# Mamba-2 mixer with a mixture-of-experts block on one core: z and output projections as three split products, one convolution tap moved from DVE to ACT and POOL, a new order on every engine

## The chip, the core and the metric

The kernel runs on one core of a Trainium2 chip. A time is the device time of one execution in microseconds (us); several executions are given by their median. The profile is of one execution. PE is TensorE (matmul), PEld its weight load, DVE is VectorE, ACT is ScalarE, POOL is GpSimd and SP is SyncE, which here only issues transfers.

## The reference, cut to what matters

Four sequences of 2048 tokens, 512 wide. A layer norm with a modulation, a Mamba-2 mixer (in-projection, a convolution of four taps, a chunked state-space scan of 16 heads, a gate, an out-projection), a second layer norm, and 64 experts of which each token takes eight, with a shared expert.

```python
h = _layernorm(x) * (1 + ca) + sa
# mixer
xn = h * rsqrt(mean(h * h) + EPS) * norm_w
zxbcdt = einsum("bld,ed->ble", xn, in_proj_w)      # z: 1024, xBC: 1024 + 128 + 128, dt: 16
conv = sum(pad[:, k:k + l, :] * conv_w[:, k] for k in range(4)) + conv_b
xBC = conv * sigmoid(conv)
dt = softplus(dt + dt_bias)
y = _ssd(xh * dt[..., None], dt * A, Bm, Cm) + D * xh       # chunks of 128 tokens
y = y * (z * sigmoid(z))
y = y * rsqrt(mean(y * y) + EPS) * gnorm_w
x = x + ga * (h + einsum("bld,ed->ble", y, out_proj_w))
# feed-forward
h = _layernorm(x) * (1 + cb) + sb
x = x + gb * (routed_experts(h) + shared_expert(h))
```

All inputs and outputs are float32.

## The kernel before

The program has three parts, each an unrolled loop or a loop over blocks of 128 tokens: `mixer` (64 chunks of 128 tokens), `experts` (576 blocks) and `combine` (64 blocks). The change touches `mixer` alone.

`mixer` is a software pipeline written by hand. A step `s` works on several chunks at a time: chunk `e = s + 2` gets its first layer norm, chunk `f = s + 1` its in-projection, convolution and gate, chunk `c = s` its scan and out-projection, chunk `t = s - 1` its second layer norm and its routing, and chunk `q = s - 2` has its token numbers scattered to the experts' lists (eight indirect DMAs that POOL issues). Each engine has a function `step` that issues its instructions for all of these chunks in the written order; nothing reorders them. Engines wait for each other by the semaphores in `S`. So a step takes as long as the slowest loop through the engines' queues, and the mixer takes about 64 such steps.

One step on each engine, in its written order:

- PE: the small products of `c` (L766 to L769), the transposes of `xr` (L775), the row sums of the decay matrix `lm` (L788), the xBC projection (L811, 40 matmuls) with the transposes of `h2` for routing (L795) in it, dt (L815), the router (L825), the scan (L832, L844, L853), the z projection (L860, eight float32 matmuls of 512 columns), the transposes of `y` (L867), the ranks, the transposes of `xbc` (L881) and the out-projection (L888, eight float32 matmuls of 512 columns).
- DVE: the residual `x1` and its statistics (L1109 to L1119, written at the end of `step`, but they run at the turn of a step), the small scan terms (L940, L944), `x1s` (L949), the decay matrix times C·B (L956), half of the splitting of the expert weights (`split_lo`, L518), three taps of the convolution for ten tiles (L982, 30 instructions), dt (L991, L993), the routing (L998 to L1037) with the terms of the softplus series between its instructions, the chain of `y` and the state (L1043 to L1056), `xbc` (L1059), gates and places, and `split_lo` again.
- POOL: `xg` (L587, L590), the two norms' powers and their scalings (L594 to L621), the elementwise products of the scan (L601, L627, L633), and the eight list DMAs (L645).
- ACT: copies from PSUM, exponentials, the first tap (L701), tanh, the upper halves of the expert weights (`split_hi`).

In the experts, and only there, a product is made of float32 operands that are split into an upper and a lower part of the type float32r: `split_products` adds hi·hi, hi·lo and lo·hi, three matmuls for one.

Of the kernel before, what the change touches and what calls it, by code (L numbers as in the profile page):

```python
# [4 lines left out]
FP32 = mybir.dt.float32  # L5
# [19 lines left out]
DIN = 2 * DI + 2 * P + NH  # L25
EXPERTS, TOPK, FF = 64, 8, 256
# [134 lines left out]
def mixer(nc, top, sem, tile, bank, half, env):  # L161
# [11 lines left out]
    with ExitStack() as ph:  # L173
# [9 lines left out]
        a_neg = sb("a_neg", [P, NH])  # L183
        d_skip = sb("d_skip", [P, NH])
# [25 lines left out]
        with ExitStack() as st:  # L210
# [7 lines left out]
            pad_id = tile(st, "pad_id", [P, P], I32)  # L218
            w_mod_dh = w_mod_d.rearrange("p k (a n) -> p k a n", a=2)
# [8 lines left out]
                     (w_router, w_router_d), (b_router, b_router_d), (w_in, w_in_d)]  # L228
            with nc.Block() as block:
                @block.sync  # L230
                def _(sp):
                    sp.dma_start(c_in[:], c_t).then_inc(s_cin, 16)
                    for a in range(2):
                        if a:
                            for dst, src in loads:
                                sp.dma_start(dst[:], src).then_inc(s_load, 16)
                            sp.wait_ge(s_pe_set, 3)
                        sp.dma_start(w_mod[:].rearrange("p k a n -> p k (a n)"),
                                     w_mod_dh[:, :, a, :]).then_inc(s_wmod[a], 16)
                    sp.dma_start(w_out[:], w_out_d).then_inc(s_wout, 16)  # L240
# [5 lines left out]
                    sp.wait_ge(s_row, 16)  # L246
                    for b in range(2):
                        sp.dma_start(mod[:, b, :, :].rearrange("p m d -> p (m d)"),
                                     mod_dram[b:b + 1, 0:5 * DM].broadcast_to([P, 5 * DM])).then_inc(s_bcast, 16)
                    sp.wait_ge(s_bcast, 16 * 2)  # L250
# [43 lines left out]
                def _(act):  # L294
                    act.wait_ge(s_const, 8)
                    act.dma_start(h2_dram[TOKENS:TOKENS + P, :], zeros[:]).then_inc(s_zero, 16)
                    act.wait_ge(s_cin, 16)
                    nc.scalar.activation(c_tanh[:], c_in[:], ACT.Tanh, scale=0.5).then_inc(s_act_set, 1)
                    act.wait_ge(s_load, 16 * len(loads))
# [5 lines left out]
                    for k in range(KD):  # L305
                        nc.scalar.activation(w_in[:, k, 0:DIN // 2], w_in[:, k, 0:DIN // 2], ACT.Copy,
                                             scale=norm_w[:, k:k + 1]).then_inc(s_act_set, 1)
                    act.wait_ge(s_wout, 16)
                    for k in range(KI):
                        nc.scalar.activation(w_out[:, k, :], w_out[:, k, :], ACT.Copy,  # L310
# [14 lines left out]
                def _(dve):  # L325
# [13 lines left out]
                    for k in range(KD):  # L339
                        nc.vector.tensor_scalar(w_in[:, k, DIN // 2:DIN], w_in[:, k, DIN // 2:DIN],  # L340
                                                norm_w[:, k:k + 1], None, ALU.mult)
# [25 lines left out]
                    nc.vector.tensor_copy(mod_abs[:, 0:1], mod_row[:, 0, 0:1]).then_inc(s_setup, 1)  # L367

        RT = 3 * P
        XGROUPS = 4  # L370
        OLD = TAPS - 1
        passed = sem("passed")
        SH_A, SC_A, G_A, SH_B, SC_B = range(5)
# [10 lines left out]
        junk = sb("junk", [P, DI], mybir.dt.bfloat16)  # L384
# [6 lines left out]
        xbc = sb("xbc", [P, 2, NE, P])  # L391
        gz = sb("gz", [P, 2, DI])
# [23 lines left out]
        y_t = sb("y_t", [P, KI, P])  # L416
# [1301 lines left out]
```

## Time and profile before

| | |
|---|---|
| median of 3 runs | 5845.8 us (5838.91 to 5846.02) |
| profiled execution, its own time | 5848.36 us |
| its span, first to last instruction | 5846.6 us |
| mean granted TensorE clock | 0.986 of full speed |
| busy, share of the span | PE 96%, PEld 73%, DVE 62%, POOL 60%, ACT 45% |

The mixer fills the first 2700 us or so, the experts most of the rest. In the mixer DVE and PE are both nearly always busy; in the experts PE is, and DVE falls to four tenths. A share over the whole span therefore says little on the mixer, and the rows further down are taken from single steps of it. A step is there about 40 us long. "Busy" on DVE or POOL includes time in which an instruction has been started and is held up, so a long duration of a short instruction is a wait too.

### The profile page before, as it was taken

Reading aid. Unit: us, or ns where it says so; the run is one execution under the profiler, and the core shown is the slowest. Engines: PE = TensorE matmul, PEld = TensorE weight load, DVE = VectorE, ACT = ScalarE, POOL = GpSimd, SP = SyncE. Lnnn points to the kernel's source line nnn. Section 1 sums busy time; section 2 is a strip of 40 time slices with the busy share of each in tenths; the row PEclk is TensorE's granted clock in tenths of the full one; section 3 lists DMA queues with packets and bytes.
Section 4 is the critical chain, followed back from the end, with each engine's and each line's share of the span. In section 5 each row is a group of like instructions: output and inputs, shape, how many; then the busy total and the mean of one; then the engine's idle time right before and its main releaser. Section 6 shows DMA issues by size and latency. Waiting matters only on the chain.

```text
span 5846.6 us, 109797 instructions
## 1 busy us (share of the span) xinstructions
PE 5613.9 (96%) x28797; PEld 4286.0 (73%) x28798; DVE 3597.2 (62%) x10033; ACT 2627.2 (45%) x5588; POOL 3535.2 (60%) x2980
## 2 busy tenths in 40 slices
PE   5999999999999999994999999999999999999999
PEld 3666666666666666663888888887888888888887
DVE  4889888888898898883444444443444444444454
ACT  3555555555555555551333333333333333333322
POOL 2667667667676676673555555554555555555587
PEclk8999999999999999996999999999999999999999
DMA  5443444444444444343688788778678778878687
GB/s 203 163 149 144 162 155 152 154 143 163 158 145 165 147 146 160 145 151 133 138 225 222 183 202 224 164 177 238 138 182 203 160 161 218 208 199 201 132 277 248
DMA packets 340193, 1028.38 MB, mean 176 GB/s; under 512 B 57109, under 2 KB 61461, under 8 KB 339173
## 3 DMA queue, kind: packets, MB, share of 16 engines
q1 hardware_dynamic: 194232, 703.53, 32.9%
q0 software_dynamic: 145568, 321.56, 28.1%
q8 instruction: 118, 1.93, 0.1%
q14 instruction: 131, 1.07, 0.1%
q10 hardware_dynamic: 144, 0.29, 0.0%
HBM read 580.45 MB, written 444.74 MB: 175 GB/s over the span
## 4 chain that ended last, share of the span: by engine, by line
PE 52%; DMA 1%; POOL 0%; issue 0%; DVE 0%; SPq 0%; ACT 0%; POOLq 0%; ACTq 0%
PE bank L1244 45%; PE bank L1379 4%; PE bank L1386 2%; PE bank L1573 0%; PE bank L1582 0%; DMA w_lo<-lo_dram 0%; POOL acc_c L1555 0%; DMA h_c<-h_dram 0%; DMA lst_i<-list_dram,row 0%; DMA xg_e<-h_dram,ids 0%; POOL o_c L1559 0%; POOL acc_c L1546 0%; DMA acc_dram<-y_e,ids 0%; POOL lst_i L1172 0%; SPq L1531 0%
## 5 line engine op out<-in xcount | busy, mean ns | idle before, releaser
L1360 POOL DMA_INDIRECT acc_dram<-y_e,ids x576 | 910.4, 1580 | 1113.1 <-ACT y_e L1432 789.1
L1244 PE MATMUL bank<-w_hi,x_hi 128*128 (+1 forms) x2560 | 1056.1, 413 | 1.7 <-DVE x_lo L1647 1.2
L1244 PE MATMUL bank<-w_hi,x_lo 128*128 (+1 forms) x2560 | 1000.8, 391 | 0.0
L1244 PE MATMUL bank<-w_lo,x_hi 128*128 (+1 forms) x2560 | 1000.7, 391 | 0.0
L1450 DVE TENSOR_TENSOR h_lo<-bank,h_hi 128x256 fp32r<-128x256 f32 x576 | 243.8, 423 | 763.9 <-ACT h_hi L1421 763.7
L1432 ACT ACTIVATE y_e<-bank,xg_e 128x512 f32<-128x512 f32 x576 | 396.4, 688 | 698.4 <-PE bank L1244 698.4
L645 POOL DMA_INDIRECT list_dram<-tok_id,pos x512 | 594.9, 1162 | 156.0 <-issue 154.8
L1352 POOL DMA_INDIRECT xg_e<-h_dram,ids x576 | 571.0, 991 | 193.9 <-issue 174.9
L1426 ACT ACTIVATE th_f<-bank 128x256 f32<-128x256 f32 x576 | 221.3, 384 | 1011.2 <-PE bank L1244 1011.2
L811 PEld LDWEIGHTS bank<-xn_t,w_in 128*128 128x128 f32 x5120 | 587.8, 190 | 67.0 <-ACT btok L687 65.4
L811 PE MATMUL bank<-xn_t,w_in 128*128 128x131 f32 x5120 | 605.4, 276 | 14.8 <-ACT btok L687 14.1
L1459 DVE SCALAR_TENSOR_TENSOR hs_f<-th_f,bank 128x256 f32<-128x256 f32 x576 | 242.7, 421 | 600.1 <-ACT th_f L1426 599.8
L1244 PEld LDWEIGHTS bank<-w_hi,x_lo 128*128 128x128 f32 x2560 | 481.3, 188 | 103.5
L1244 PEld LDWEIGHTS bank<-w_hi,x_hi 128*128 128x128 f32 x2560 | 482.8, 189 | 83.4 <-DVE x_lo L1647 1.4
L1244 PEld LDWEIGHTS bank<-w_lo,x_hi 128*128 128x128 f32 x2560 | 484.1, 189 | 79.1
L982 DVE SCALAR_TENSOR_TENSOR acc<-bank,conv_w,acc 128x128 f32<-128x128 f32 x1920 | 505.7, 341 | 8.5 <-ACT acc L701 8.4
L1244 PE MATMUL bank<-w_hi,h_hi 128*128 (+1 forms) x1280 | 499.5, 390 | 2.2 <-DVE h_lo L1450 1.3
L1244 PE MATMUL bank<-w_hi,h_lo 128*128 (+1 forms) x1280 | 500.0, 391 | 0.0
L1244 PE MATMUL bank<-w_lo,h_hi 128*128 (+1 forms) x1280 | 498.1, 389 | 0.0
L888 PE MATMUL bank<-w_out,y_t 128*128 128x512 f32 x1024 | 452.4, 595 | 1.2 <-ACT y_t L751 1.2
L860 PE MATMUL bank<-w_in,xn_t 128*128 128x512 f32 x1024 | 450.0, 592 | 0.9 <-DVE acc L982 0.9
L1455 DVE TENSOR_TENSOR x_lo<-bank,x_hi 128x512 fp32r<-128x512 f32 x576 | 392.1, 681 | 8.7 <-ACT x_hi L1416 8.7
(247 smaller groups left out, 10448.6 us busy)
## 6 DMA issues: line engine op xcount, KB each, us to landing
hi_dram<-w_hi_m SPq DMA_DIRECT2D x130, 768.0 KB, 3.3
lo_dram<-w_raw SPq DMA_DIRECT2D x130, 768.0 KB, 4.8
w_hi<-hi_dram SPq DMA_DIRECT2D x130, 768.0 KB, 7.4
w_lo<-lo_dram SPq DMA_DIRECT2D x130, 768.0 KB, 10.2
w_raw<-in_w_experts_dram SPq DMA_DIRECT2D x128, 768.0 KB, 5.0
acc_dram<-zeros SPq DMA_DIRECT2D x130, 256.0 KB, 2.8
acc_c<-acc_dram SPq DMA_DIRECT2D x128, 256.0 KB, 3.5
h_dram<-h SPq DMA_DIRECT2D x64, 288.0 KB, 4.1
```

Of the source, the lines that this page charges most:

```text
L645: pool.indirect_dma_start(list_dram, bass.IndirectOffsetOnAxis(ap=pos[:, p, k:k + 1], axis=0), tok_id[:, p:p + 1], None).then_inc(list_st[ ...
L811: last = nc.tensor.matmul(raw_of(i), w_in[:, k, m:m + P], xn_t[:, k, :], start=(k == 0), stop=(k == KD - 1))
L860: last = nc.tensor.matmul(half(j), xn_t[:, k, OLD:], w_in[:, k, j * 512:(j + 1) * 512], start=(k == 0), stop=(k == KD - 1))
L888: last = nc.tensor.matmul(half(7), y_t[:, i, :], w_out[:, i, :], start=(i == 0), stop=(i == KI - 1))
L982: last = stt(out=acc[:, i, :], in0=raw_of(i)[:, k:k + P], scalar=conv_w[:, i, k:k + 1], in1=acc[:, i, :], op0=ALU.mult, op1=ALU.add)
L1244: last = nc.tensor.matmul(acc, a, b, start=(i == 0), stop=(i == len(terms) - 1))
L1352: pool.indirect_dma_start(xg[:, r, :], None, h2_dram, bass.IndirectOffsetOnAxis(ap=ids[:, r:r + 1], axis=0)).then_inc(g_in[r], 16)
L1360: pool.indirect_dma_start(acc_dram[r % NACC], bass.IndirectOffsetOnAxis(ap=ids[:, r:r + 1], axis=0), y[:, r % YSLOTS, :], None, compute_op ...
L1432: nc.scalar.activation(y[:, r % YSLOTS, :], half(6 + r % 2), ACT.Copy, scale=xg_flat[:, bass.ds(e + (r * ROW + DM), 1)]).then_inc(S["y_sb" ...
L1450: nc.vector.tensor_tensor(h_lo[:, r, :], half(4 + r)[:, 0:KF * P], h_hi[:, r, :].bitcast(FP32), ALU.subtract).then_inc(S["hT_lo"], 1)
L1455: nc.vector.tensor_tensor(x_lo[:, r, :], half(r), x_hi[:, r, :].bitcast(FP32), ALU.subtract).then_inc(S["xT_lo"], 1)
L1459: nc.vector.scalar_tensor_tensor(out=hs[:, r, :], in0=th[:, r, :], scalar=1.0, in1=half(2 + r)[:, 0:FF], op0=ALU.add, op1=ALU.mult).then_i ...
```

## The change

z and output projections. The weights of z and of the output are split once, at the start, into `wz_hi`, `wz_lo`, `wo_hi`, `wo_lo`; each step splits `xn` and `y` (upper part copied by ACT, lower part subtracted by DVE), and PE multiplies by three float32r matmuls in place of each float32 one: 48 in place of 16 in a step.

Convolution. DVE's three taps become two. ACT multiplies the second tap into a new tile `acc2` (ten more instructions in a step) and POOL adds `acc2` to `acc` (one instruction of 128x1280).

Order and buffers. The small products and terms of a chunk move from the start of its step to the end of the one before. The residual `x1` moves to the start of the next step. The C·B matrix goes into an SBUF tile `cbm`, where before it stayed in PSUM. `xbc` and `gz` have one buffer in place of two, `y` lies in `acc2`, `y_hi` and `y_lo` share memory with `x1s` and `x2s`, `tmp_s` is gone (POOL scales `state` in place). The modulation rows lie in three tiles of which two are loaded for one batch at a time; the zeros for the accumulators are read from a 128x128 tile by a repeating pattern; both halves of the weight splitting stand at the end of a step on DVE.

```diff
@@ ACT, convolution, one group of four @@
-                        for i in group(g):
-                            last = nc.scalar.activation(acc[:, i, :], raw_of(i)[:, 0:P], ACT.Identity,
-                                                        bias=conv_b[:, i:i + 1], scale=conv_w[:, i, 0:1])
+                        for i in group(0):
+                            nc.scalar.activation(acc2[:, i, :], raw_of(i)[:, 1:1 + P], ACT.Copy, scale=conv_w[:, i, 1:2])
+                            last = nc.scalar.activation(acc[:, i, :], raw_of(i)[:, 0:P], ACT.Identity, bias=conv_b[:, i:i + 1], scale=conv_w[:, i, 0:1])
...
@@ POOL @@
+                        pool.wait_ge(S["taps"], XGROUPS * (f + 1))
+                        nc.gpsimd.tensor_tensor(acc[:], acc[:], acc2[:], ALU.add).then_inc(S["csum_done"], 1)
...
-                        nc.gpsimd.tensor_tensor(heads(tmp_s[:]), heads(state[:]), per_head(etk[:]),
-                                                ALU.mult).then_inc(S["tmps_done"], 1)
+                        pool.wait_ge(S["yoff_ps"], c + 1)
+                        nc.gpsimd.tensor_tensor(heads(state[:]), heads(state[:]), per_head(etk[:]), ALU.mult).then_inc(S["tmps_done"], 1)
@@ PE @@
-                        for j in range(2):
-                            pe.wait_ge(S["taps"], XGROUPS * f + 2 - j)
-                            for k in range(KD):
-                                last = nc.tensor.matmul(half(j), xn_t[:, k, OLD:], w_in[:, k, j * 512:(j + 1) * 512],
-                                                        start=(k == 0), stop=(k == KD - 1))
-                            last.then_inc(S["z_ps"], 1)
+                        pe.wait_ge(S["taps"], XGROUPS * f + 2)
+                        pe.wait_ge(S["xn_lo"], f + 1)
+                        split_products(nc, half(0), [lambda k, t=t: t[:, k, :] for t in (xn_hi, xn_lo)],
+                                       [lambda k, t=t: t[:, k, 0:512] for t in (wz_hi, wz_lo)], KD).then_inc(S["z_ps"], 1)
...
-                        for i in range(KI):
-                            last = nc.tensor.matmul(half(7), y_t[:, i, :], w_out[:, i, :], start=(i == 0), stop=(i == KI - 1))
-                        last.then_inc(S["out_ps"], 1)
+                        first = [(y_hi, k, w) for k in range(KI) for w in (wo_hi, wo_lo)]
+                        for i, (a, k, w) in enumerate(first):
+                            nc.tensor.matmul(half(7), a[:, k, :], w[:, k, :], start=(i == 0), stop=False)
...
+                        pe.wait_ge(S["ylo_done"], c + 1)
+                        for k in range(KI):
+                            last = nc.tensor.matmul(half(7), y_lo[:, k, :], wo_hi[:, k, :], start=False, stop=(k == KI - 1))
+                        last.then_inc(S["out_ps"], 1)
@@ DVE @@
+                        tt(xn_lo[:], xn_t[:, :, OLD:], xn_hi[:].bitcast(FP32), ALU.subtract).then_inc(S["xn_lo"], 1)
...
-                            tt(heads(lm[:, j * DI:(j + 1) * DI], 8, P), heads(lm[:, j * DI:(j + 1) * DI], 8, P),
-                               half(4)[:, 0:P].unsqueeze(1).to_broadcast([P, 8, P]), ALU.mult).then_inc(S["m_done"], 1)
+                        tt(heads(lm[:, 0:DI], 8, P), heads(lm[:, 0:DI], 8, P),
+                           cbm[:].unsqueeze(1).to_broadcast([P, 8, P]), ALU.mult).then_inc(S["m_done"], 1)
...
-                            for k in range(1, TAPS):
+                        for k in range(K1, TAPS):
...
+                        if c + 1 < NCH:
+                            dve.wait_ge(S["csum_done"], c + 2)
...
+                        tt(y_lo[:].rearrange("p k t -> p (k t)"), bank[2][:], y_hi[:].rearrange("p k t -> p (k t)").bitcast(FP32), ALU.subtract).then_inc(S["ylo_done"], 1)
```

In the order of the instructions two places matter. The first is POOL's queue from the first power of a step to its list DMAs; `ve` and `mv` are the norms' statistics from DVE, `pos` are the places from the routing. Before:

```order
L587 TENSOR_TENSOR xg<-h,mod 128x512 [waits h_done,x1_done]
L590 TENSOR_TENSOR xg<-xg,xin 128x512 [waits x_in0,xg_half]
L594 TENSOR_TENSOR rs<-ve,minus_half 128x1 [waits hn2_done,ln2_var]
...
L619 TENSOR_TENSOR h<-hn,mod 128x512 [waits xr_done,hn_done]
L621 TENSOR_TENSOR h<-h,mod 128x512 [waits h_half]
L627 TENSOR_TENSOR x2s<-x1s,eacs 128x1024 [waits states_ps,exps,x1s_done]
L633 TENSOR_TENSOR tmp_s<-state,etk 128x1024 [waits state_done,etk_done]
L638 TENSOR_SCALAR rre<-ssq 128x1 [waits ssq_done]
L640 TENSOR_TENSOR rr<-rre,minus_half 128x1 [waits rr_var]
L645 DMA list_dram<-tok_id,pos 540672x1 [waits pos_done]
```

And with the change, from the list DMAs of one step to the last large product of the next:

```order
L697 DMA list_dram<-tok_id,pos 540672x1 x7
L632 TENSOR_TENSOR rs<-ve,minus_half 128x1 [waits hn2_done,ln2_var]
...
L647 TENSOR_TENSOR h<-hn,mod_b 128x512 [waits h2T_ps,h2_st0,hn2_done]
L649 TENSOR_TENSOR h<-h,mod_b 128x512 [waits h2_half]
L652 TENSOR_TENSOR xt<-xt,d_skip 128x1024 [waits x1s_done]
L657 TENSOR_TENSOR x2s<-x1s,eacs 128x1024 [waits states_ps,out_ps,exps,x1s_done]
L663 TENSOR_TENSOR xg<-h,mod_g 128x512 [waits h_done,x1_done]
L666 TENSOR_TENSOR xg<-xg,xin 128x512 [waits x_in0,xg_half]
L668 TENSOR_TENSOR acc<-acc 128x1280 [waits taps]
L673 TENSOR_TENSOR state<-state,etk 128x1024 [waits yoff_ps,state_done,etk_done]
L680 TENSOR_TENSOR h<-hn,mod_a 128x512 [waits xg_half,xr_done,hn_done]
L682 TENSOR_TENSOR h<-h,mod_a 128x512 [waits h_half]
```

`xg` moved from the head of the queue to behind `x2s`, the sum of the taps stands behind it and waits for DVE's last tap, the scaling of the state waits for PE's `yoff`, and the scalings of `h` for the first norm come last.

The second place is DVE's queue between the first norm's statistics and the routing. Before (`split_lo` is the row on `w_raw`):

```order
L949 TENSOR_TENSOR x1s<-xt,dt 128x1024 [waits x2s_done,dt_done,xt_sb]
L952 TENSOR_SCALAR etk<-eacs,ends 128x16 [waits tmps_done,exps]
L956 TENSOR_TENSOR lm<-lm,bank 128x1024 [waits l_exp] x2
L961 BN_STATS st<-xin 128x6 [waits x_in1]
L964 BN_AGGR mv<-st 128x2 [waits ln1_stat,dve_e]
L966 TENSOR_SCALAR ve<-mv 128x1 [waits dve_e]
L518 TENSOR_TENSOR w_raw<-w_raw,w_hi_m 128x1536 [waits w_hi]
L982 SCALAR_TENSOR_TENSOR acc<-bank,conv_w,acc 128x128 [waits tap0]
```

With the change:

```order
L1040 TENSOR_SCALAR ve<-mv 128x1 [waits dve_e]
L1045 TENSOR_TENSOR xn_lo<-xn_t,xn_hi 128x512 [waits z_ps,xn_hi]
L1049 TENSOR_TENSOR lm<-lm,cbm 128x1024 [waits cb_done,l_exp]
L1056 TENSOR_TENSOR x1s<-xt,dt 128x1024 [waits ydiag_ps,x2s_done,out_ps,dt_done,xt_sb]
L1066 SCALAR_TENSOR_TENSOR acc<-bank,conv_w,acc 128x128 [waits tap0]
...
L1075 TENSOR_TENSOR lm<-lm,cbm 128x1024 [waits cb_done,l_exp]
L1079 TENSOR_SCALAR etk<-eacs,ends 128x16 [waits tmps_done,exps]
L1083 TENSOR_TENSOR sp_x<-bank,dt_bias 128x16 [waits tap0]
L1085 SCALAR_TENSOR_TENSOR sp_a<-sp_x 128x16 [waits dt_raw]
L1093 SCALAR_TENSOR_TENSOR acc<-bank,conv_w,acc 128x128 [waits tap0]
```

The products with C·B read `cbm` in place of a PSUM bank and stand apart, `xn_lo` is new, `split_lo` has left this stretch for the end of the step, and the two taps that are left are 20 instructions in two pieces.

## Rows read from the trace of the kernel before

**Rows 1.** PE in one step of the mixer: start, duration, line, tiles, idle before.

```profile
1508.24 1.09 PE L867 MATMUL bank<-ident,y 128*128 128x128 f32 x8 [0.62 <-DVE y L1056]
...
1509.64 1.09 PE L881 MATMUL bank<-ident,xbc 128*128 128x128 f32 x8 [0.25 <-DVE xbc L1059]
1510.57 7.03 PE L888 MATMUL bank<-w_out,y_t 128*128 128x512 f32 x16
1517.44 0.38 PE L766 MATMUL bank<-xbc 128*128 128x128 f32 x2
...
1522.43 8.37 PE L811 MATMUL bank<-xn_t,w_in 128*128 128x131 f32 x72 [0.22 <-ACT btok L687]
...
1548.42 1.09 PE L867 MATMUL bank<-ident,y 128*128 128x128 f32 x8 [0.63 <-DVE y L1056]
```

**Rows 2.** PE in one block of the experts: split products, 512 columns each.

```profile
4004.80 0.39 PE L1244 MATMUL bank<-w_lo,x_hi 128*128 x1
...
4008.46 0.39 PE L1244 MATMUL bank<-w_hi,h_lo 128*128 x1
```

**Rows 3.** Waits of DVE from 1000 to 1400 us: total, times, longest.

```profile
DVE x L1109 <- PE bank L888: 27.2, 10, 2.7
```

**Rows 4.** DVE by line, 1000 to 1400 us, ten steps: busy, mean ns, idle before.

```profile
L982 DVE SCALAR_TENSOR_TENSOR acc<-bank,conv_w,acc 128x128 f32<-128x128 f32 x300 | 79.0, 341 | 0.0
L518 DVE TENSOR_TENSOR w_raw<-w_raw,w_hi_m 128x1536 fp32r<-128x1536 f32 x20 | 36.2, 1812 | 0.0
L956 DVE TENSOR_TENSOR lm<-lm,bank 128x1024 f32<-128x1024 f32 x20 | 23.5, 1218 | 2.0 <-ACT lm L691 2.0
L1047 DVE TENSOR_TENSOR y<-y,bank 128x1024 f32<-128x1024 f32 x10 | 12.2, 1222 | 1.1
L1111 DVE TENSOR_TENSOR x<-x,xg 128x512 f32<-128x512 f32 x10 | 6.9, 692 | 0.3
```

**Rows 5.** DVE and POOL side by side in one step: start, duration.

```profile
1520.55 1.26 POOL L590 TENSOR_TENSOR xg<-xg,xin 128x512 f32<-128x512 f32 x1
...
1520.83 1.02 DVE L944 TENSOR_TENSOR acs<-acs 128x16 f32<-128x16 f32 x1
...
1526.70 1.87 DVE L518 TENSOR_TENSOR w_raw<-w_raw,w_hi_m 128x1536 fp32r<-128x1536 f32 x1
1527.03 2.67 POOL L609 TENSOR_TENSOR h<-h,mod 128x512 f32<-128x512 f32 x1
...
1536.06 1.90 POOL L633 TENSOR_TENSOR tmp_s<-state,etk 128x1024 f32<-128x1024 f32 x1
...
1536.51 1.48 DVE L993 SCALAR_TENSOR_TENSOR sp_a<-sp_x 128x16 f32<-128x16 f32 x1
```

**Rows 6.** POOL by line, 1000 to 1400 us, ten steps.

```profile
L645 POOL DMA_INDIRECT list_dram<-tok_id,pos x80 | 93.2, 1166 | 24.8 <-issue 24.8
L601 POOL TENSOR_TENSOR xt<-xt,d_skip 128x1024 f32<-128x1024 f32 x10 | 19.0, 1904 | 0.0
L613 POOL TENSOR_TENSOR rs<-ve,minus_half 128x1 f32<-128x1 f32 x10 | 5.5, 546 | 0.0
```

**Rows 7.** The routing, the chain of y and the end of a step.

```profile
1537.91 0.18 DVE L998 TENSOR_SCALAR sc<-trt 128x64 f32<-128x64 f32 x1
...
1539.10 1.08 POOL L645 DMA_INDIRECT list_dram<-tok_id,pos  x1 [0.18 <-issue]
...
1542.30 1.21 DVE L1043 TENSOR_TENSOR y<-bank,eacs 128x1024 f32<-128x1024 f32 x1
...
1548.28 1.49 DVE L1059 SCALAR_TENSOR_TENSOR xbc<-xbc,acc 128x1280 f32<-128x1280 f32 x1
...
1553.34 1.75 DVE L518 TENSOR_TENSOR w_raw<-w_raw,w_hi_m 128x1536 fp32r<-128x1536 f32 x1
```

**Rows 8.** Mixer's last steps, by stretch: PE, PEld, DVE, ACT, POOL busy, PEclk, DMA, GB/s.

```profile
2650.20:2653.80 3.60, 0.00 (x0) 0.00 (x0) 2.26 (x2) 0.00 (x0) 3.52 (x3) 0.51 0.37 152
2653.80:2667.30 13.50, 12.79 (x48) 10.76 (x49) 3.49 (x24) 2.17 (x3) 11.20 (x10) 0.50 0.26 100
```

More of the change, by code:

```diff
@@ L183, in mixer @@
         a_neg = sb("a_neg", [P, NH])
+        cbm = sb("cbm", [P, P])
         d_skip = sb("d_skip", [P, NH])
@@ L733, in step @@
                     if f is not None:
[L734 to L736 removed]
+                        act.wait_ge(S["z_ps"], 2 * f + 2)
+                        nc.scalar.activation(gz[:, 512:1024], half(1), ACT.Tanh, scale=0.5).then_inc(S["z_th"], 1)
                     if e is not None:
@@ L792, in transposes @@
+                    if c is not None:
+                        pe.wait_ge(S["xt_sb"], c + 1)
+                        pe.wait_ge(S["l_in"], 2 * c + 2)
+                        for i in range(2):
+                            at = DI + i * 512
+                            last = nc.tensor.matmul(half(2 + i), above[:], lm[:, at:at + 512], start=True, stop=True)
+                        last.then_inc(S["rows_ps"], 1)
+                    if t is not None:
                         pe.wait_ge(S["h2_done"], t + 1)
@@ new lines, in step @@
+                        for k in range(K1, TAPS):
+                            for hf in range(2):
+                                if k == K1:
+                                    dve.wait_ge(S["tap0"], XGROUPS * f + hf + 1)
+                                else:
+                                    conv.wait(2 * (k - K1 - 1) + hf + 1)
+                                for i in group(hf):
+                                    last = stt(out=acc[:, i, :], in0=raw_of(i)[:, k:k + P], scalar=conv_w[:, i, k:k + 1],
+                                               in1=acc[:, i, :], op0=ALU.mult, op1=ALU.add)
+                                if k == TAPS - 1:
+                                    last.then_inc(S["taps"], 1)
+                                else:
+                                    conv.mark(last)
@@ L1074, in step @@
                     if f is not None:
+                        for n in range(0 if t is None else SERIES_IN_ROUTE, SERIES):
+                            series(n)
+                        dve.wait_ge(S["z_th"], 2 * f + 1)
+                        stt(out=gz[:, 0:512], in0=gz[:, 0:512], scalar=1.0,
+                            in1=half(0), op0=ALU.add, op1=ALU.mult).then_inc(S["gz_done"], 1)
                         softplus.wait()
```

660 lines of the change are left out of this document (378 added, 282 removed).

## Prediction

> **What bounds the kernel now.** The page says that PE is busy 96% of the span, but that is an average over two stages, so I went to one step of the mixer. On PE the reader is to see how little is missing: the transposes of `y` start at 1508.24 and again at 1548.42, a step of 40.18 us, and PE waits in it for 0.62 + 0.25 + 0.22 = 1.09 us [rows 1]. Next come DVE's waits: it waits in each step 2.72 us for the out-projection, and for nothing else that counts [rows 3]. So a step is one loop through both engines: PE's out-projection, DVE's long queue from `x1` to the chain of `y`, PE's transposes. DVE has 40.18 - 2.72 = 37.46 us of it, PE 39.09.
>
> Last I laid DVE and POOL side by side, since DVE's own time holds hidden waits [rows 5]. `acs` is 16 columns wide and takes 1.02 us: it is over at 1521.85, and the POOL addition beside it, from SBUF, at 1521.81. `sp_a`, as small, takes 1.48 and is over at 1537.99, POOL's product at 1537.96. In the other direction POOL's 512-column addition L609 takes 2.67 where L590, of the same form, takes 1.26: it starts under `split_lo`, which ends at 1528.57, and needs 1.13 more. All these DVE instructions read two SBUF operands. The taps, which read one from PSUM, run in those very microseconds undisturbed: 79.0/300 = 0.263 each [rows 4]. So two-SBUF instructions of DVE and POOL's products exclude each other for a whole instruction, either way. Before, this costs DVE (1.02 - 0.18) + (1.48 - 0.18) = 2.14 us a step, taking the 0.18 of `sc` as a small instruction's price. It costs no more because the routing, with its many small two-SBUF instructions, starts at 1537.91, and POOL turns to the list DMAs at 1539.10 [rows 7]; routing and the chain of `y` run under these.
>
> **The change part by part.**
>
> PE. In the experts 16 split products in a row start 3.66 us apart, 0.229 each [rows 2], so three are 0.686. The eight float32 products take 1517.44 - 1510.57 = 6.87, 0.859 each [rows 1]. Sixteen are replaced: 16 x 0.173 = 2.8 us. PE's loop is then 39.09 - 2.8 = 36.3.
>
> DVE, undisturbed: 37.46 - 2.14 = 35.3. Ten taps less are -2.63 [rows 4]. `xn_lo` costs 0.69 as the `x1` addition, `y_lo` 1.22 as the like-shaped addition from PSUM [rows 4]. For the small terms, now behind 16 matmuls of the out-projection (3.66), and one more dependent pair in the chain of `y`, I add 0.8, an estimate between 0.3 and 1.5. That gives 35.4. Were nothing else to happen, a step would be 36.3 to 36.8.
>
> POOL. `tmp_s` becomes `state`, same size, and the sum of the taps is new: 1.90 x 1280/1024 = 2.38 [rows 6]. Its queue now cannot start its products before DVE has the second norm's variance, since that norm's power is first behind the list DMAs. From that moment, call it 0, POOL has to do: four small steps of the norms 1.6 (0.55 a power), six 512-column products 7.6 (1.26 each), three of 1024 columns 5.7, the sum 2.4; 17.3, with some 1.2 between them 18.5 [rows 5, 6]. DVE undisturbed would from 0 do statistics (about 1.1), `xn_lo` 0.7, `lm` 1.2, `x1s` 1.2, twelve taps 3.2, `lm` 1.2, small ones 0.6, eight taps 2.1, and reach the routing at 11.3. The routing is 4.4 long (1537.91 to 1542.30 [rows 7]) and would be done at 15.7. So POOL is still multiplying in all of it.
>
> The price of that. `xn_lo`, two `lm` and `x1s` are 4.3 us of two-SBUF work that cannot lie beside POOL's 18.5; the two `lm` are new in this, since C·B lay in PSUM and now lies in `cbm`. POOL is then done at up to 22.8. The routing and the series between its instructions need the port eleven times (scores, group sums, comparisons, masks, weights, six of the series). Each of these waits for the POOL instruction in progress, and gets in between two of them. In the eight or so POOL instructions left, about five of the eleven get through; what is left, 2.0 us, follows. The routing ends at 24.8 in place of 15.7: 9.1 lost. If DVE gets on better, so that POOL is kept off for half of the 4.3 and only 1.0 is left over, it ends at 21.7: 6.0 lost. I take 8.4, nearer to the upper end, because in each of [rows 5] the loser waits for the whole instruction. The Trainium skill has this in "SBUF — State Buffer", section "Who interferes with whom": a DVE instruction with two SBUF inputs contends with a GpSimd instruction that reads SBUF, whichever comes second stands still until the first is done, and one with at most one SBUF input does not contend. The trace agrees (0.84 and 1.30 lost beside 0 for the taps). It also condemns the `lm` products, of which no row shows a conflict, since they had a PSUM operand. Without them in it the loss would be 8.4 - 2.4 = 6.0, and the time near 6100.
>
> The clock. PE's loop of 36.3 then has 7 us of waiting in a step of 43.8, most of it in one piece before the transposes of `y`, where it waits for DVE today [rows 1]. In the mixer's tail, where PE stands still for 3.6 us, it is granted 0.51 there and 0.50 in the 13.5 us of work that follow [rows 8], the lower of its two levels, 1.2 GHz. From the transposes of `y` to the small products PE has 2.3 + 3.7 = 6 us of work, and DVE waits for these. Cost: nothing, if the clock is back at once, to 6.0, if it stays down all this way; I take 2.7.
>
> ACT gets eleven instructions more, and is the idlest of the compute engines over the span (45%); SP's transfers, the four times smaller pieces of the zeros, two splittings at the start (8 x 0.69 on DVE, beside the load of the modulation rows) and one more empty step I set at nothing. If that cover fails, they cost some 10 us once.
>
> Sum: 35.4 + 8.4 + 2.7 = 46.5 us a step in place of 40.18, +6.3. About 63 of the 68 steps are full ones: +398 on the profiled execution's own 5848.4 (it is 2.6 above the median shown), so 6246, say 6250.
>
> **The rivals.**
>
> Port without clock: 43.8 a step, +3.6, 6075. For it: PE's work after an idle piece may be spread enough for the clock to come back early. Against: [rows 8].
>
> Faster, the port bites less. Only instructions that meet a long POOL product wait (the second `lm` behind `xt`, `sp_a` behind `x2s`: some 1.4 + 1.5, and 0.6 elsewhere), and the routing slips between POOL's instructions. Then 38.9 a step, -1.3, 5766. It decides at a loss of 40.18 - 35.4 = 4.8 us a step: under that the change is faster. For it: no row shows the routing beside POOL products. Against: `acs` and `sp_a` are as small as the routing's instructions and waited.
>
> Faster, PE's loop alone bounds: the holds stay as small as today's in total, DVE keeps ahead, 36.8 a step, -3.4, 5634. For it: DVE's undisturbed 35.4 is under PE's 36.3. Against: POOL's 18.5 us from moment 0 are longer than DVE's 15.7.
>
> Slower still: the clock stays down for the whole 6.0 us, and the loss is the full 9.1: 50.5, 6500.
>
> **How the numbers follow.** Port and clock 0.50 (on its own 6100 to 6420), port without clock 0.20, the port bites less 0.10, PE alone 0.15, slower still 0.05. A measurement tells about 0.2%, 12 us, from no change. The faster cases give 0.08 of the 0.10 and all of the 0.15: 0.23; same 0.02; slower 0.75. The range leaves out PE alone and the slowest, 0.20: 5760 to 6420.
>
> **What the profile of the changed kernel would show.** If right: small instructions of the routing and the series (`swb`, `gs`, `sp_s`, `sp_q`, `gcmp`) on DVE with durations near 1 us or more, ending together with POOL's `acc`, `state` or `h`; `lm` or POOL's products lengthened by the other; PE waiting some microseconds for `y`; the granted clock under 1.00 through the mixer; steps of 44 to 48 us. The split products should start 0.23 us apart at full clock, whichever case it is. If DVE's small instructions stay near 0.2 us and PE's waits under 1 us a step, the port was not the point and I am wrong by some 600 us. Wrong, too, if POOL's products are over before the routing starts: then moment 0 is earlier than I put it.

## The result and the profile after

| | before | after |
|---|---|---|
| median | 5843.8 us (5838.91 to 5846.02, 4 runs) | 6284.0 us (6278.31 to 6289.44, 4 runs) |
| ratio | | 1.0754, 95% interval 1.0736 to 1.0773 |
| span of the profiled execution | 5846.6 us | 6285.6 us |
| mean granted TensorE clock | 0.986 | 0.937 |

The median before has one run more than the one further up. One run of the versions below, 6250 us with the skip product on ACT, counts as slow and is left out of its median and its ratio.

The change costs 440 us. The page's rows of busy time and of the granted clock, after:

```profile
PE 5643.3 (90%) x29821; PEld 4635.8 (74%) x29822; DVE 3961.6 (63%) x9533; ACT 2829.9 (45%) x6356; POOL 3821.8 (61%) x3044
PEclk8989989989888998998889999999999999999999
```

DVE and POOL are as busy as before, in share; PE's share has fallen from 96% to 90%, and the clock is under full in the first half, the mixer. To see where the time lies, take DVE's product for `xbc`, which stands once in each step. The columns are count, duration in ns (least, median, longest), first and last start. First before, then after:

```profile
L1059 DVE SCALAR_TENSOR_TENSOR xbc<-xbc,acc x64: 1481/1484/1493, 99.0 to 2633.6; 128x1280 f32<-128x1280 f32 x64
```

```profile
L1167 DVE SCALAR_TENSOR_TENSOR xbc<-xbc,acc x64: 1476/1484/2579, 94.8 to 3077.0; 128x1280 f32<-128x1280 f32 x64
```

64 starts are 63 steps: (2633.6 - 99.0)/63 = 40.23 us before, (3077.0 - 94.8)/63 = 47.34 after. 63 x 7.11 = 448 us; behind the last step both kernels need 3213 and 3209 us. So all of the loss is in the mixer's step. (Steps of the kernels below are worked out in the same way.)

Three of the 63 steps, where a new sequence begins, take 53.3, 52.6 and 53.9 us; the other 60 take 47.04 on the mean. In each of the three POOL's `h` waits for the modulation rows of the new sequence (total, times, longest wait):

```profile
POOL h L647 <- DMA mod_b<-mod_dram: 19.7, 3, 7.7
```

They make up 19 us of the 448. The kernel before has no step over 40.7 us behind its second.

In one step, DVE from its wait for the small products into the routing (start, duration, idle before):

```profile
1512.18 0.19 DVE L1218 COPY acs<-bank 128x32 f32<-128x32 f32 x1 [3.73 <-PE bank L965]
...
1519.05 0.15 DVE L1031 TENSOR_SCALAR ve<-mv 128x1 f32<-128x1 f32 x1
...
1527.18 1.60 DVE L1075 TENSOR_TENSOR lm<-lm,cbm 128x1024 f32<-128x1024 f32 x1 [0.87 <-ACT lm L771]
1528.70 1.87 DVE L1079 TENSOR_SCALAR etk<-eacs,ends 128x16 f32<-128x16 f32 x1
...
1533.79 0.18 DVE L1103 TENSOR_SCALAR sc<-trt 128x64 f32<-128x64 f32 x1
1534.00 2.91 DVE L1105 TENSOR_TENSOR swb<-sc,b_router 128x64 f32<-128x64 f32 x1
1536.84 1.89 DVE L992 TENSOR_SCALAR sp_r<-sp_u 128x16 f32<-128x16 f32 x1
...
1540.22 1.13 DVE L998 TENSOR_TENSOR sp_s<-sp_u,sp_r 128x16 f32<-128x16 f32 x1
...
1544.03 1.23 DVE L1152 TENSOR_TENSOR acc<-bank,eacs 128x1024 f32<-128x1024 f32 x1
```

And POOL in the same stretch of time:

```profile
1519.29 0.57 POOL L632 TENSOR_TENSOR rs<-ve,minus_half 128x1 f32<-128x1 f32 x1 [1.87 <-DVE ve L1031]
...
1527.66 2.88 POOL L657 TENSOR_TENSOR x2s<-x1s,eacs 128x1024 f32<-128x1024 f32 x1
...
1533.94 2.89 POOL L668 TENSOR_TENSOR acc<-acc 128x1280 f32<-128x1280 f32 x1 [0.84 <-DVE acc L1093]
1536.79 1.90 POOL L673 TENSOR_TENSOR state<-state,etk 128x1024 f32<-128x1024 f32 x1
...
1540.03 1.28 POOL L682 TENSOR_TENSOR h<-h,mod_a 128x512 f32<-128x512 f32 x1
```

Add start and duration to see which instructions end together. `etk` is over at 1530.57, POOL's `x2s` at 1530.54. `swb`, 64 columns wide, takes 2.91 and is over at 1536.91, the sum of the taps at 1536.83. `sp_r` is over at 1538.73, `state` at 1538.69; `sp_s` at 1541.35, `h` at 1541.31. The routing, 4.4 us before [rows 7], takes 1544.03 - 1533.79 = 10.2.

The groups of DVE's lines from 1000 to 1400 us (count, busy, mean ns) say that every step is like that:

```profile
L1105 DVE TENSOR_TENSOR swb<-sc,b_router 128x64 f32<-128x64 f32 x9 | 26.2, 2910 | 0.3
L1079 DVE TENSOR_SCALAR etk<-eacs,ends 128x16 f32<-128x16 f32 x9 | 16.8, 1867 | 0.0
L1075 DVE TENSOR_TENSOR lm<-lm,cbm 128x1024 f32<-128x1024 f32 x9 | 14.4, 1601 | 7.8 <-ACT lm L771 7.8
L992 DVE TENSOR_SCALAR sp_r<-sp_u 128x16 f32<-128x16 f32 x9 | 13.5, 1504 | 0.0
L1085 DVE SCALAR_TENSOR_TENSOR sp_a<-sp_x 128x16 f32<-128x16 f32 x9 | 10.0, 1116 | 0.3
L998 DVE TENSOR_TENSOR sp_s<-sp_u,sp_r 128x16 f32<-128x16 f32 x9 | 9.6, 1067 | 0.0
L1112 DVE TENSOR_TENSOR gs<-g 128x8 f32<-128x8 f32 x9 | 8.1, 896 | 0.3
L1121 DVE CAST gidf<-gidx 128x8 f32<-128x8 uint32 x9 | 3.7, 407 | 0.0
```

The time that such an instruction takes beyond its own price is called a hold here. With 0.18 us as the price of a small instruction and 1.22 of `lm`, the means give 2.73 + 1.69 + 0.38 + 1.32 + 0.94 + 0.89 + 0.72 + 0.23 = 8.9 us of holds in a step, 2.1 before.

The waits of the same stretch (total, times, longest):

```profile
ACT gz L803 <- DVE acc L1161: 76.3, 8, 9.7
POOL rre L685 <- ACT hn L808: 72.7, 8, 9.3
...
PE bank L937 <- DVE state L1164: 53.8, 8, 7.2
...
DVE acs L1218 <- PE bank L965: 24.9, 8, 3.8
```

The two largest, of ACT and POOL, end with the chain of `y`; ACT's is at the tile `gz`, which has one buffer now. Whether anyone is held up by them is tried below. PE waits 53.8/8 = 6.7 us a step for `y` and the state, DVE 24.9/8 = 3.1 for the small products behind PE's transposes. PE by stretches of one step (length, busy of PE, PEld, DVE, ACT, POOL, then the granted clock):

```profile
1495.50:1502.80 7.30, 0.00 (x0) 0.01 (x1) 6.75 (x11) 1.17 (x3) 0.00 (x0) 0.71 0.00 1
1502.80:1508.80 6.00, 5.98 (x24) 5.45 (x25) 5.30 (x19) 5.20 (x10) 4.72 (x7) 0.51 0.26 96
1508.80:1513.90 5.10, 5.10 (x27) 4.21 (x27) 1.72 (x4) 4.16 (x15) 3.88 (x5) 1.00 0.05 2
```

PE stands still for 7.3 us; the next 6.0, the transposes and the first part of the out-projection, are granted 0.51, the lower level, and then it is back at 1.00.

### The profile page after: what moved, and what is told of

Same layout as the page of the kernel before. It is cut to its first block and busy times, and to the rows that moved or that the text cites. A ratio compares the mean times of both kernels' runs of the same rounds, so it can differ in the third digit from the quotient of the medians.

```text
span 6285.6 us, 113210 instructions
## 1 busy us (share of the span) xinstructions
PE 5643.3 (90%) x29821; PEld 4635.8 (74%) x29822; DVE 3961.6 (63%) x9533; ACT 2829.9 (45%) x6356; POOL 3821.8 (61%) x3044
## 5 line engine op out<-in xcount | busy, mean ns | idle before, releaser
L697 POOL DMA_INDIRECT list_dram<-tok_id,pos x512 | 619.7, 1210 | 155.8 <-issue 154.7
L937 PE MATMUL bank<-ident,acc 128*128 128x128 f32 x512 | 118.7, 410 | 390.4 <-DVE state L1164 390.4
L937 PEld LDWEIGHTS bank<-ident,acc 128*128 128x128 f32 x512 | 95.9, 215 | 416.9 <-issue 416.9
L685 POOL TENSOR_SCALAR rre<-ssq 128x1 f32<-128x1 f32 x64 | 69.4, 1085 | 535.0 <-ACT hn L808 535.0
L1527 ACT CAST x_hi<-bank 128x512 fp32r<-128x512 f32 x576 | 332.8, 578 | 67.5 <-PE bank L1490 67.4
L1490 PE MATMUL bank<-ident,xg_e 128*128 128x128 f32 x2304 | 346.6, 273 | 17.7 <-SPq L1443 8.0
## 6 DMA issues: line engine op xcount, KB each, us to landing
w_lo<-lo_dram SPq DMA_DIRECT2D x130, 768.0 KB, 10.2
```

What stands on the lines that cost most here:

```text
L697: pool.indirect_dma_start(list_dram, bass.IndirectOffsetOnAxis(ap=pos[:, p, k:k + 1], axis=0), tok_id[:, p:p + 1], None).then_inc(list_st[ ...
L937: last = nc.tensor.transpose(bank[2][:, i * P:(i + 1) * P], y[:, i * P:(i + 1) * P], ident[:])
L1490: last = nc.tensor.transpose(half(r % 2)[:, k * P:(k + 1) * P], xg[:, r, k * P:(k + 1) * P], ident[:])
L1527: nc.scalar.copy(x_hi[:, r, :], half(r)).then_inc(S["xT_hi"], 1)
```

## The experiments

Theory: DVE and POOL hold each other up, since POOL's products now reach into the routing (8.9 us a step), and PE's idle piece costs half the clock (2 to 3 us). Rivals: the single buffers and the waits on them; DVE's mere amount of work; the split products on PE. All edits are made to the changed kernel. In the cuts of the edits below `...` stands for lines left out. What was measured, the ratios against the kernel before, the step of the profiled execution:

| edit | median us | ratio, 95% interval | us a step |
|---|---|---|---|
| none (the change) | 6284.0 | 1.0736 to 1.0773 | 47.34 |
| gate tile in two buffers | 6287.7 | 1.0742 to 1.0777 | 47.32 |
| list DMAs earlier | 6289.1 | 1.0750 to 1.0786 | 47.28 |
| POOL's products cut short | 6079.2 | 1.0384 to 1.0419 | 44.17 |
| sum of the taps on DVE | 6212.2 | 1.0616 to 1.0651 | 46.13 |
| second tap back on DVE | 6148.5 | 1.0504 to 1.0539 | 45.03 |
| sum on DVE, state on ACT | 6113.0 | 1.0442 to 1.0477 | 44.52 |
| the same, skip product on ACT | 6154.8 | 1.0468 to 1.0536 | 45.62 |
| sum on DVE, C·B in PSUM, lists earlier | 6138.6 | 1.0489 to 1.0525 | 44.97 |
| tap on DVE, C·B in PSUM, lists earlier | 6299.5 | 1.0762 to 1.0798 | 47.66 |
| PE's idle time filled | 6331.6 | 1.0817 to 1.0853 | 48.01 |
| z in float32 | 6315.5 | 1.0791 to 1.0827 | 47.74 |
| tap on DVE, state on ACT, small terms off the port | 6079.9 | 1.0380 to 1.0415 | 44.17 |

**The rivals first.** The gate tile in two buffers:

```diff
-        gz = sb("gz", [P, DI])
+        gz = sb("gz", [P, 3, 512])
...
-                        at_least(act, S["y_done"], f)
-                        nc.scalar.activation(gz[:, 0:512], half(0), ACT.Tanh, scale=0.5).then_inc(S["z_th"], 1)
+                        at_least(act, S["y_done"], f - 1)
+                        nc.scalar.activation(gz[:, p, :], half(0), ACT.Tanh, scale=0.5).then_inc(S["z_th"], 1)
...
```

> The first half of the gate tile gz gets a second buffer again, so that ACT's tanh into it does not wait for the product of y with the gate (9.5 us a step in the changed kernel), and POOL not for ACT behind it (9.3 us); xr lies in hn to make room, and DVE's product y x gate is two instructions of 512 columns. Port theory: these waits end with the chain of y and hold nobody up, 6284 us, 25 more or less. Theory of the single buffers: 2 us a step or more come back, under 6160 us.

6288: no change. ACT's wait is now at the next instruction that needs `y`, 6.8 us a step for 9.5, POOL's is 7.0 for 9.1, and PE waits as before:

```profile
POOL r2e L690 <- ACT hn L814: 56.1, 8, 7.3
PE bank L940 <- DVE state L1168: 54.1, 8, 7.1
ACT hn L814 <- DVE acc L1165: 54.1, 8, 7.0
```

So more than 2 us of these waits went and nothing was gained: that buffer is not the cause. (Of the other shared buffers none was tried alone.) The list DMAs, moved from the end of POOL's step to behind `h`:

> POOL's eight list DMAs of a step move from its end to behind the last large product h (as before the change, where they ran under the routing). Port theory: POOL's products still cannot start before moment 0 and are as long, so the routing still lies beside them: 6284 us, 60 more or less. Rival, that the routing is only held because the list DMAs left it and pushed the products into it: the holds go, 4 us a step or more, under 6040 us.

6289: no change. POOL then waits for the second norm's variance 94.3/9 = 10.5 us a step, where it waited 0.8: its products can't start sooner, whatever stands ahead of them.

**POOL's products in the routing.** First both made short: the sum is made for one tile of ten, the scaling of the state for one head of sixteen, and the rest of both is left out:

```diff
-nc.gpsimd.tensor_tensor(acc[:], acc[:], acc2[:], ALU.add).then_inc(S["csum_done"], 1)
+nc.gpsimd.tensor_tensor(acc[:, 0:1, :], acc[:, 0:1, :], acc2[:, 0:1, :], ALU.add).then_inc(S["csum_done"], 1)
...
-nc.gpsimd.tensor_tensor(heads(state[:]), heads(state[:]), per_head(etk[:]), ALU.mult).then_inc(S["tmps_done"], 1)
+nc.gpsimd.tensor_tensor(heads(state[:])[:, 0:1, :], heads(state[:])[:, 0:1, :], per_head(etk[:])[:, 0:1, :], ALU.mult).then_inc(S["tmps_done"], 1)
```

> Two POOL instructions are cut short: the sum of the taps is made for one tile of ten, and the scaling of the state for one head of sixteen (that part of the convolution and of the state is left out). POOL loses about 4.4 us of product time in the routing. Port theory: the holds of swb (2.7) and sp_r (1.7) go and those behind h come earlier; 4 to 6 us a step less, 5900 to 6040 us. Theory of the single buffers or of the waits on ACT: no change above 1 us a step, 6220 us or more.

3.2 us a step came back, less than the 4 to 6 expected, and far more than the rival's 1. DVE's instructions are the same ones. Then work was moved without leaving any out. The sum behind DVE's last tap:

```diff
-                        nc.gpsimd.tensor_tensor(acc[:], acc[:], acc2[:], ALU.add).then_inc(S["csum_done"], 1)
...
+                        dve.wait_ge(S["taps"], XGROUPS * (f + 1))
+                        tt(acc[:], acc[:], acc2[:], ALU.add).then_inc(S["csum_done"], 1)
```

> The sum of the two tap tiles (128x1280) is made by DVE behind its last tap, not by POOL. Port theory: DVE gets about 1.5 us of work, but the hold of swb (2.7 us, ended by that POOL sum) goes, and POOL's later products end about 2.5 us earlier against the routing, so that part of the other holds (sp_r 1.7, gs 0.5, sp_s 1.0) goes too: 1 to 4 us a step less, 6030 to 6220 us. Theory that DVE's amount of work decides: 1.5 us a step more, about 6380 us. Theory of the single buffers: 6284 within 20 us or a little more.

DVE does 1.5 us more, and the step is 1.2 us shorter. `swb` is a small instruction again:

```profile
L1099 DVE TENSOR_TENSOR acc<-acc 128x1280 f32<-128x1280 f32 x8 | 11.9, 1492 | 0.3
L1105 DVE TENSOR_TENSOR swb<-sc,b_router 128x64 f32<-128x64 f32 x8 | 1.8, 226 | 0.3
```

The convolution put back whole (`K1 = 1`, no `acc2` product, no sum):

> Only the convolution is put back: the second tap on DVE (ten instructions of 0.26 us that read PSUM), no second tap tile on ACT and no sum on POOL. Port theory: DVE's own work is 2.6 us longer, and of the 9.3 us of holds a step the 2.7 under the sum and part of those behind it go, as with the sum on DVE (6.2 us of holds left there, 46.1 us a step): 44.5 to 47 us a step, 6105 to 6265 us. Theory that only DVE's amount of work counts: 2.6 us a step more than the changed kernel, 6450 us.

6149: DVE has ten instructions of 0.26 us more, and the step is 2.3 us shorter. That DVE's amount of work decides is refuted twice. Next, with the sum on DVE, the state's scaling went to ACT as well:

```diff
...
+                        for hh in range(NH):
+                            last = nc.scalar.activation(state[:, hh * HD:(hh + 1) * HD], state[:, hh * HD:(hh + 1) * HD], ACT.Copy, scale=etk[:, hh:hh + 1])
+                        last.then_inc(S["tmps_done"], 1)
```

> The sum of the taps on DVE, and the scaling of the state by ACT instead of POOL (16 instructions of 128x64, behind the convolution's tanh, where ACT waits 9.5 us for y). Port theory: the 1.9 us that POOL's product of the state held DVE's routing go as well; against the kernel with the sum on DVE (46.1 a step, 6212) 1.5 to 3 us a step less, 6020 to 6120 us. Theory that DVE's small instructions are slow for another reason than POOL: no change, 6212 or, through ACT's 4 us more work, above.

6113, as expected. The rows of DVE from 1000 to 1400 us:

```profile
L1079 DVE TENSOR_SCALAR etk<-eacs,ends 128x16 f32<-128x16 f32 x9 | 16.8, 1868 | 0.0
L1101 DVE TENSOR_TENSOR acc<-acc 128x1280 f32<-128x1280 f32 x9 | 16.0, 1783 | 0.3
...
L1105 DVE TENSOR_SCALAR sc<-trt 128x64 f32<-128x64 f32 x9 | 11.3, 1259 | 0.0
...
L1107 DVE TENSOR_TENSOR swb<-sc,b_router 128x64 f32<-128x64 f32 x9 | 2.0, 225 | 0.3
...
L992 DVE TENSOR_SCALAR sp_r<-sp_u 128x16 f32<-128x16 f32 x9 | 1.5, 167 | 0.0
L998 DVE TENSOR_TENSOR sp_s<-sp_u,sp_r 128x16 f32<-128x16 f32 x9 | 1.4, 157 | 0.0
```

`swb`, `sp_r` and `sp_s` are free; `etk`, which stands beside `x2s`, has not moved, and POOL's `h` now meets the sum (1.78 for 1.49) and `sc` (1.26 for 0.18). The holds follow POOL's products from line to line. Then the skip product, `xt` times `d_skip`, went to ACT too:

> As the last one, and the product of xt with the skip weights goes to ACT too (16 more instructions). POOL has then 11 to 12 us of products and norms from moment 0, and 4.3 us of DVE's two-SBUF work beside them; DVE comes to the routing 12.8 us after moment 0. Port theory: few holds are left in the routing (under 3 us a step), TensorE's wait before the transposes of y shrinks to 1 to 3 us: 40 to 42.6 us a step, 5840 to 6000 us, near the kernel before or under it. If ACT's 8 us become the new wait: 44 us a step or more, 6080 us.

6155, with runs from 6121 to 6180. The mean of 45.6 us a step hides two kinds of steps. In the profiled execution 34 of the 63 take 42.0 to 43.8 us, at or near the first case of the expectation, and 25 take 47.8 to 48.3. One of each (length, busy times, clock as above):

```profile
1059.81:1101.85 42.04, 38.11 (x225) 31.23 (x225) 37.19 (x100) 33.81 (x93) 24.78 (x23) 0.95 0.43 145
500.59:548.60 48.01, 43.16 (x225) 35.12 (x225) 37.51 (x101) 33.62 (x93) 25.87 (x23) 0.86 0.42 127
```

In the longer one PE's products with `lm` run at half clock, 7.06 us where after has 3.74. So the scan behind them reaches ACT late, ACT's 32 products for `xt` and the state come late too, and DVE waits 2.7 us for `xt` and 1.3 for the state. From 1016 to 1360 us, where all steps are of the shorter kind, DVE waits for neither. So it is not ACT's work by itself that costs the time.

**C·B in PSUM.** With the lists earlier and the sum on DVE, and with three more waits that keep PE and ACT off C·B's PSUM bank while DVE reads it:

```diff
-tt(cbm[:], half(4)[:, 0:P], tri[:], ALU.mult).then_inc(S["cb_done"], 1)
+tt(half(4)[:, 0:P], half(4)[:, 0:P], tri[:], ALU.mult).then_inc(S["cb_done"], 1)
```

> Together: list DMAs behind h, the sum of the taps on DVE, and C·B masked in place in PSUM, so that the two lm products read one SBUF operand (three waits keep PE and ACT off that PSUM bank while DVE reads it). Port theory: the sum on DVE gave 1.2 us a step (6212), the lm products cost up to 2.4 us of exclusion: 1 to 2.5 us more, 6050 to 6150 us. Theory that the lm products do not matter: 6212 within 25 us.

> As the last one, but the second tap is back on DVE (ten instructions of 0.26 us with an operand in PSUM, which POOL did not disturb before the change), ACT makes no second tap tile and nobody sums. Port theory: DVE works 2.6 us in place of 1.5, but without a two-SBUF instruction, and ACT's conv is 10 instructions shorter: about as the last one, 6050 to 6200 us. Theory that DVE's work decides: 1.1 us a step over the last one, 70 us.

The first gave 6139, 74 us under the sum on DVE alone, as expected; C·B in PSUM by itself was not measured, so how much of it the earlier lists brought stays open. The second, with the tap in place of the sum, is a miss: 6300. Its small instructions are held for only some 2.5 us a step, by the reckoning above, and the time went into other waits:

```profile
ACT xr L823 <- POOL rr L692: 43.6, 8, 8.2
...
PE bank L834 <- ACT xr L823: 20.8, 5, 4.2
```

Its steps take about 45 us or about 50, mostly by turns. In a shorter one PE waits 1.9 us for `lm`, by one of the three new waits, and its products with `lm` run at half clock (6.71 us); POOL's product of the state then waits 9.8 us for the scan, and the list DMAs start late. In the longer one behind it they stand ahead of POOL's `rr`, `xr` waits for that, and PE's transposes of it for `xr`. In the same place they had cost nothing while POOL was waiting anyway.

**The clock.** The second half of z made three times over, so that PE works in its idle piece:

> The second half of the z product is issued three times over, so that TensorE works where it stood idle before the transposes of y; its result is the same. In the changed kernel DVE waits 3.1 us a step for the small products behind those transposes, 0.5 before the change. Port and clock theory: the half clock there comes from the idle piece of 7.2 us; 24 more matmuls of 0.229 us fill 5.5 of it, the granted clock is 1.00 in the mixer, the transposes of y take 1.1 in place of 1.9, the wait falls to about 0.5, the step from 47.6 to about 45, the time to about 6120 us (6080 to 6200). The holds on DVE stay. Theory of the single buffers: no change, 6284 within 20 us. Theory that the split products themselves cost the time on TensorE: 5.5 us a step more, 6600 us or above.

All theories missed it: 6332. What was to be shown is there, and something else too (one step; lengths, busy times, clock as above):

```profile
1532.95:1540.00 7.05, 6.86 (x42) 5.93 (x43) 5.29 (x19) 6.94 (x16) 5.49 (x7) 1.00 0.25 83
1559.58:1569.60 10.02, 10.02 (x37) 7.95 (x38) 9.75 (x35) 0.22 (x1) 5.12 (x3) 0.52 0.28 106
```

```profile
1532.95 1.06 PE L939 MATMUL bank<-ident,acc 128*128 128x128 f32 x8 [0.75 <-DVE state L1166]
...
1540.00 0.19 DVE L1220 COPY acs<-bank 128x32 f32<-128x32 f32 x1 [1.41 <-PE bank L967]
...
1559.58 6.70 PE L902 MATMUL bank<-x1s,lm 128*128 128x64 f32 x32 [1.22 <-DVE lm L1077]
```

The transposes of `y` run at full clock, and DVE waits 1.41 us for the small products in this step, 3.73 in the step shown of after. So the half clock there costs 2.3. But in the same step PE waits 1.22 us for `lm`, and from there on 10.0 us are granted 0.52: the loss has moved to the products with `lm`, and in the next step PE, with 5.5 us of filling to do, ends after `y` is there and is on the path. That `lm` is late has to do with holds again: POOL's `nm`, one column wide, takes 2.38 us and ends with DVE's `x1s`, ACT's `hn` waits for it, and DVE's taps wait 1.97 us for ACT.

**z in float32**, with the rest left as changed:

> The z product alone is made as before the change, by eight float32 matmuls of 512 columns in place of 24 split ones, with the upper parts of its weights as its weights (the lower parts are left out); ACT does not copy and DVE does not subtract for xn. Theory that DVE's chain with its holds sets the step, and that TensorE's saving is nobody's: 8 x 0.17 = 1.4 us more on TensorE fall into its 7.2 us of idle time, the 0.69 us of xn_lo come off DVE, and 0 to 0.5 more with them: 0.5 to 1.2 us a step less, 6205 to 6255 us. Theory that what the split saves on TensorE is worth its time: 1.4 us a step more, 6370 us.

6315: between the two, and both miss. Two rows of DVE show part of what became of the 0.69 us of `xn_lo`, `lm` taking 2.94 where it took 1.60:

```profile
L1070 DVE TENSOR_TENSOR lm<-lm,cbm 128x1024 f32<-128x1024 f32 x8 | 23.5, 2940 | 9.6 <-ACT lm L768 9.6
...
L1074 DVE TENSOR_SCALAR etk<-eacs,ends 128x16 f32<-128x16 f32 x8 | 9.9, 1232 | 0.0
```

DVE comes to it no earlier, 7.9 us behind POOL's first power in a step of either kernel, since it waits 1.2 us for ACT's exponentials where it waited 0.9. POOL is half a microsecond further, so that `lm` meets the whole of `x2s` and not the end of `xt`. By the reckoning above the holds are 10.2 us for 8.9. Here too PE waits 1.2 us a step for `lm`, and its products with it take 353 ns on the mean for 275; how the 0.4 us that the step grew by divide between the two was not tried. Nor was the out-projection put back into float32.

**All of it together**, the tap on DVE, the state on ACT, `etk` made by ACT, and `sp_a` with one operand from PSUM:

```diff
...
-                        ts(etk[:], eacs[:, NH:2 * NH], col(ends, c), None, ALU.mult).then_inc(S["etk_done"], 1)
+                        nc.scalar.activation(etk[:], eacs[:, NH:2 * NH], ACT.Copy, scale=col(ends, c)).then_inc(S["etk_done"], 1)
```

> The second tap back on DVE, the state scaled by ACT, and the two small DVE instructions that POOL still holds taken from the port: etk made by ACT, and sp_a read from PSUM and one SBUF operand (for which dt is summed in place in PSUM and copied, one more small instruction). Port theory: against the kernel with the tap back (45.0 a step, 6149), the holds of etk 1.3 and sp_a 1.0 go, etk's own 0.2 too, and of those in the routing and the chain of y, which POOL's product of the state makes, about 1.5: 41 a step, 40 to 42, 5835 to 5965 us. If the holds only move on to the next two-SBUF instruction: 43.5 or more, 6050 us or above.

6080: the second case of the expectation. The holds on `etk` and `sp_a` went, `lm` and `swb` took over part of them, and the clock is now in the path:

```profile
L1074 DVE TENSOR_TENSOR lm<-lm,cbm 128x1024 f32<-128x1024 f32 x10 | 25.8, 2578 | 0.0
L1103 DVE TENSOR_TENSOR swb<-sc,b_router 128x64 f32<-128x64 f32 x9 | 12.1, 1342 | 0.3
```

```profile
1224.69:1231.54 6.85, 6.85 (x32) 6.85 (x33) 6.62 (x34) 0.22 (x1) 4.75 (x4) 0.50 0.44 152
889.79:931.82 42.03, 37.27 (x229) 30.11 (x227) 38.16 (x109) 28.80 (x70) 27.84 (x24) 1.00 0.44 145
```

In the first of these stretches PE, which waited 1.6 us for `lm` before it, runs its 32 products at half clock, 7.06 us for 3.74 in after; before the transposes of `y` it no longer waits at all. The second is a whole step at full clock. Four of the 63 steps are like it and take 41.5 to 42.0 us, where most others take 44.4: so full clock is worth about 2.4 us a step here. It still holds `lm`, `sc` and `swb` for 2 us together and is 1.8 us over a step before. No version came under the kernel before, and none was free of both the holds and the half clock.

## Why the prediction was right

It said 6250, 5760 to 6420, slower with 0.75; 6284 was measured. By its steps:

- **Moment 0 and POOL's 18.5 to 22.8 us.** Right at the upper end. In the step shown the variance is there at 1519.20, POOL's last `h` over at 1541.31: 22.1 us. It is held itself (`x2s` 2.88 for 1.90, the second `nm` 1.70 for 0.27), and the sum takes 2.89 where 2.38 was put.
- **The routing begins at 11.3 and ends at 24.1 to 24.8.** The end is right, the beginning is not: it begins 14.6 us after moment 0 and ends after 24.8. Ahead of it lie 3.0 us of holds (`lm`, `etk`, `sp_a`) that the prediction had put into the routing, and DVE's 0.87 us of waiting for ACT's exponentials ahead of `lm`, which it did not have. The routing itself lost 5.8 us, 10.2 for 4.4.
- **Holds, 8.4 us lost.** 8.9 were measured. The mechanism is right; that the amount is so near is in part luck, since 8.4 was a choice between 6.0 and 9.1. That POOL's products make them is shown for those in the routing (`swb`, `sp_r`, `sp_s` go with the sum and the state); for `etk` beside `x2s` only the ends agree, since no edit was made to try it. Which instructions are held was too narrow: `etk`, `sp_r` and the conversion `gidf` read one tensor from SBUF, not two, and account for 3.2 of it.
- **Clock, 2.7 us.** The place was right and the price near: 2.3, from one step of each kernel. That it comes of PE's idle piece agrees with the full clock behind the filled piece. It is not an amount that can be had back alone, as the filling showed. That the clock could fall at a second place, at the products with `lm`, the prediction did not have; in after these take 275 ns on the mean from 1000 to 1400 us, full clock.
- **PE's split products, 0.23 apart, and PE no longer the bound.** Right: PE waits 6.7 us a step for `y`.
- **What was put at nothing.** The load of the modulation rows is not covered: 19 us in three steps, where the prediction had named some 10 us, once, if that cover failed.
- **The sum.** 35.4 + 8.4 + 2.7 = 46.5 a step; measured 47.34, and 47.04 without the three steps at a new sequence. With 8.9 for the holds, 2.3 for the clock and 0.9 for the unforeseen wait it is 47.5, half a microsecond over that; DVE's undisturbed 35.4 was not measured by itself. A step has grown by 7.11 and not by 6.3: 63 x 0.8 = 50 us. 6246 and 50, less 4 behind the mixer and 4 ahead of its first step, are 6288; the profiled execution's own time is 6287.5, the median 3.5 under it.
- **The rivals.** Port without clock (43.8 a step), port bites less (38.9), PE alone (36.8) and slower still (50.5) are out by the step. The turning point, 4.8 us of loss, was passed with 11.2 (8.9 and 2.3).

Its sum adds POOL's holds to DVE's work as if the two were independent. The experiments speak against it: with 0.7 us of DVE's work gone the holds grew and the step did not get shorter, and with the sum on DVE, 1.5 us of work more, `swb` and `sp_r` were free and `gidf` and the series behind it were held for longer. For the size of this change it made no difference, for what an edit brings it did.

## What to carry to other kernels

Lay the queues of DVE and POOL side by side before moving work to an idle POOL: here an instruction of 64 columns cost 2.9 us when it started under a POOL product, and a tap taken off DVE to save 2.6 us cost more than that in the routing behind it. When one such hold is taken away, look which instruction meets the product next, and whether the engine that waited has lost its clock on the way, before counting it as a gain. A wait of 9 us that ends with the last thing of a step may cost nothing; try it with a second buffer rather than sort by length. And look at the steps one by one: a mean of 45.6 us was made of steps of 42 to 44 and of 48, which the clock told apart.

## What was not expected of the hardware

DVE instructions with one SBUF tensor are held too, if they are of the kind tensor_scalar or a conversion: `etk` 1.87 us for 16 columns, `sp_r` 1.89, ending with POOL's product within 0.04 us, `sc` 1.26 on the mean in the kernel with the state on ACT. The norms' `ve`, of one column, took 0.15 also in the kernel before, where it ran beside POOL's `xg` and `h`. The Trainium skill has this in "SBUF — State Buffer", section "Who interferes with whom": copies, casts and tensor_scalar can enter modes that take the port shared with GpSimd, and whoever issues first keeps it for the whole instruction. The rows agree. The prediction had given that section's rules on two inputs and on at most one without the exception that it makes for these modes.

The clock fell at a second place, without a long standstill: 1.2 and 1.6 us of waiting for `lm`, behind a shorter wait of 0.9 and the small matmuls of dt and the router, were followed by 7 to 10 us at 0.50 to 0.52. In the version with the skip product on ACT a wait of 0.6 us for `lm`, behind others of 0.9 and 0.2, stood ahead of 7.06 us at half clock.
